# Second attention of a two-attention block: scores query-major, P turned by DMA

## The reference, cut to what matters

```python
# x: (2, 1024, 128) f32, so B = 2 batches, S = 1024 tokens, E = 128
x = x + attn_a(layernorm(x))        # 16 heads of 64, causal
x = x + ffn(layernorm(x))           # relu(h @ w1 + b1) @ w2 + b2, width 512
x = x + attn_b(layernorm(x))        # the part that the change touches
x = x + ffn(layernorm(x))           # the same weights again

def attn_b(x):                      # one head, E = 128
    scores = einsum('bqe,bke->bqk', x @ W_qk, x) / sqrt(128)
    scores = scores + (kpos - qpos) * alibi_slope          # linear bias
    scores = where(qpos >= kpos, scores, -inf)             # causal
    attn = softmax(scores, axis=-1)
    return einsum('bqk,bkd->bqd', attn, x @ W_v.T)
```

## Time and profile before

| | |
|---|---|
| median of 3 runs | 562.55 us |
| span of the profiled execution | 561.3 us |
| instructions | 17932 |
| PE busy | 526.3 us (94%) |
| DVE busy | 446.3 us (80%) |
| ACT busy | 469.0 us (84%) |
| POOL busy | 453.8 us (81%) |
| mean granted TensorE clock | 0.988 |

### The profile page before, as it was taken

The page is one execution under the profiler, slowest core; times in us unless marked ns, Lnnn a source line. Parts: engine busy times, 40 slices in busy tenths (PEclk is TensorE's granted clock), DMA queues, the critical chain, the costliest instruction groups (busy, mean ns, idle before and its releaser), DMA issues.

```text
span 561.3 us, 17932 instructions
## 1 busy us (share of the span) xinstructions
PE 526.3 (94%) x6864; PEld 371.1 (66%) x6864; DVE 446.3 (80%) x1382; ACT 469.0 (84%) x925; POOL 453.8 (81%) x447
## 2 busy tenths in 40 slices
PE   4888999999999999999999999998989998798897
PEld 3654666666666666766667666675679695656576
DVE  5878888888888888888888888887785575788943
ACT  3888998999988999989999899998973978573995
POOL 5678989888888888888888888888983977654885
PEclk9979999999999999999999999999999999998999
DMA  9442343332433324333243332435147100000002
GB/s 227 109 113 57 72 110 86 96 96 68 114 87 97 95 64 118 87 95 96 60 122 80 102 97 58 124 78 198 40 151 272 68 3 2 1 1 2 1 21 57
DMA packets 35461, 48.03 MB, mean 86 GB/s; under 512 B 10777, under 2 KB 16817, under 8 KB 35377
## 3 DMA queue, kind: packets, MB, share of 16 engines
q1 hardware_dynamic: 33264, 46.35, 30.2%
q10 hardware_dynamic: 2112, 0.54, 0.4%
HBM read 12.27 MB, written 9.44 MB: 39 GB/s over the span
## 4 chain that ended last, share of the span: by engine, by line
PE 75%; DVE 8%; issue 6%; ACT 5%; POOL 5%; DMA 1%; DVEq 0%; POOLq 0%; ACTq 0%
PE psum L562 11%; PE psum L620 10%; PE psum L621 10%; PE psum L516 7%; PE psum L518 6%; PE psum L517 6%; PE psum L600 6%; PE psum L602 6%; PE psum L601 6%; PE psum L623 2%; POOL h_lo L2146 1%; PE psum L781 1%; POOL rstd L2024 1%; ACT xn L1164 1%; DVE st_lo L1515 1%
## 5 line engine op out<-in xcount | busy, mean ns | idle before, releaser
L2079 POOL TENSOR_TENSOR p_hl<-p,p_hl 128x512 f16<-128x512 f32 x288 | 328.5, 1165 | 48.4 <-ACT p_hl L1264 44.6
L1532 DVE CUSTOM_DVE_ANT_0 max_junk<-psum,mask_s 128x1024 bf16<-128x1024 f32 (+7 forms) x256 | 190.4, 753 | 32.7 <-issue 32.6
L1263 ACT ACTIVATE p<-psum 128x512 f32<-128x512 f32 x288 | 175.9, 611 | 13.8 <-PE psum L623 12.2
L1264 ACT ACTIVATE p_hl<-psum 128x512 f16<-128x512 f32 x288 | 177.2, 615 | 0.0
L620 PE MATMUL psum<-q_hl,k_hh 128*128 128x512 f16 (+3 forms) x384 | 125.6, 327 | 0.5 <-ACT p_hl L1264 0.4
L600 PE MATMUL psum<-v_all,p_hl 128*128 128x65 f16 x1152 | 124.8, 193 | 1.1 <-POOL p_hl L2079 1.0
L601 PE MATMUL psum<-v_all,p_hl 128*128 128x64 f16 x1152 | 124.9, 192 | 0.0
L602 PE MATMUL psum<-v_all,p_hl 128*128 128x65 f16 x1152 | 124.4, 194 | 0.0
L621 PE MATMUL psum<-q_hm,k_l 128*128 128x512 f16 (+3 forms) x384 | 122.3, 327 | 0.0
L600 PEld LDWEIGHTS psum<-v_all,p_hl 128*128 128x128 f16 x1152 | 107.1, 98 | 16.1 <-POOL p_hl L2079 1.2
L601 PEld LDWEIGHTS psum<-v_all,p_hl 128*128 128x128 f16 x1152 | 106.2, 97 | 4.8
(11 more groups left out here) (206 smaller groups left out, 1109.1 us busy)
## 6 DMA issues: line engine op xcount, KB each, us to landing
k_hh<-st_hi SPq DMA_DIRECT2D x64, 128.0 KB, 2.3
o_scratch<-o_sb SPq DMA_DIRECT2D x16, 512.0 KB, 2.6
o_in<-o_scratch SPq DMA_DIRECT2D x8, 1024.0 KB, 8.6
q_hl<-st_hi SPq DMA_DIRECT2D x32, 128.0 KB, 2.4
q_hl<-st_lo SPq DMA_DIRECT2D x32, 128.0 KB, 2.4
k_l<-st_lo SPq DMA_DIRECT2D x32, 128.0 KB, 2.3
q_hm<-st_hi SPq DMA_DIRECT2D x32, 128.0 KB, 2.4
x_sb<-in_L_attn_a_x SPq DMA_DIRECT2D x4, 256.0 KB, 3.9
```

What stands on the lines that cost most here:

```text
L1263: nc.scalar.activation(p32[:, ring_at(u, r), :], src, ACT.Exp, scale=SCALE_A).then_inc(exp_done, 1)
L1264: nc.scalar.activation(p_hl[:, u % 2, 0, BANK * r:BANK * (r + 1)], src, ACT.Exp, scale=SCALE_A).then_inc(phi_done, 1)
L1532: nc.vector.tensor_tensor_reduce(out=max_junk[:, n % 2, 0:cols], in0=max_banks(v, j, 0, cols), in1=mask_s[:, S - cols:S], scale=1.0, scala ...
L2079: nc.gpsimd.tensor_tensor(p_hl[:, u % 2, 1, cols], p32[:, ring_at(u, r), :], p_hl[:, u % 2, 0, cols], ALU.subtract)\
```

## The change

The second attention makes its scores once, query-major, in three passes (row j of 128 queries against its 128(j+1) keys, in the banks of ROW_BANKS). `take_row_b` is the former reduce, but keeps its elementwise output, score plus bias, in a ring of three f32 rows (rows32); a one-column operation negates and scales the maximum. `exponentials_b` works on a row, with the negated maximum as per-partition bias and the score scale as per-partition scale: first the float16 high half into p_rows, then, in place, the f32 value. `low_b` writes the low half beside the high one, and one DMA transpose per row, issued from SP, turns both halves into pt_b, keys on the partitions. `outputs_b` reads that. The maxima pass, the transposed maxima, k_one, qm_b, bias_t and `biased` are gone. All four lists of calls are written anew for this part; the calls per engine are the same otherwise.

```diff
+    ROW_BANKS = (3, 4, 3, 4, 5, 3, 5, 3, 5, 6, 5, 6, 3, 3, 3, 3)
+    ROW_AFTER = (0, 0, 1, 2, 0, 4, 5, 6, 7, 7, 9, 10, 8, 13, 14, 15)
+    ROW_RING, MOVE_RING = 3, 4
@@ sync, between the loads of the first attention's output and the result stores
+            for m in range(B * QT):
+                j, slot = m % QT, m % MOVE_RING
+                sp.wait_ge(plob_done, m + 1)
+                sp.dma_start_transpose(pt_b[:, m // QT, j * (j + 1):(j + 1) * (j + 2), :], p_rows[:, slot, 0:2 * P * (j + 1)])\
+                    .then_inc(row_moved[slot], 16)
@@ tensor
+            def scores_b(b, j):
+                m = QT * b + j
+                if j % CT == 0:
+                    pe.wait_ge(qb_lo_done, m // CT + 1)
+                if m == 0:
+                    pe.wait_ge(ot_lo_done, OB * CHUNKS)
+                if m == CT:
+                    pe.wait_ge(h_hi_done, FW * CHUNKS)
+                if ROW_AFTER[m]:
+                    pe.wait_ge(row_done, ROW_AFTER[m])
+                rows, cols = slice(P * m, P * (m + 1)), P * (j + 1)
+                for c0 in range(0, cols, BANK):
+                    c1 = min(c0 + BANK, cols)
+                    keys = slice(S * b + c0, S * b + c1)
+                    last = three(psum[:, BANK * ROW_BANKS[m] + c0:BANK * ROW_BANKS[m] + c1], qb_hi[:, rows], qb_lo[:, rows], xT_hi[:, keys], xT_lo[:, keys])
+                last.then_inc(row_full, 1)
             def outputs_b(b, j):
-                        pe.wait_ge(plob_done, NU * b + need_units[j])
+                        pe.wait_ge(row_moved[m % MOVE_RING], 16 * (m // MOVE_RING + 1))
...
@@ scalar
+            def exponentials_b(b, j):
+                m, cols = QT * b + j, P * (j + 1)
+                slot = m % MOVE_RING
+                act.wait_ge(row_turned, m + 1)
+                if m >= MOVE_RING:
+                    act.wait_ge(row_moved[slot], 16 * (m // MOVE_RING))
+                src = rows32[:, m % ROW_RING, 0:cols]
+                nc.scalar.activation(p_rows[:, slot, 0:cols], src, ACT.Exp, bias=neg_max[:, m:m + 1], scale=score_scale[:, 0:1]).then_inc(phib_done, 1)
+                act.wait_ge(phib_done, m + 1)
+                nc.scalar.activation(src, src, ACT.Exp, bias=neg_max[:, m:m + 1], scale=score_scale[:, 0:1]).then_inc(expb_done, 1)
@@ vector
+            def take_row_b(b, j):
+                m, cols = QT * b + j, P * (j + 1)
+                dve.wait_ge(row_full, m + 1)
+                if m >= ROW_RING:
+                    dve.wait_ge(plob_done, m - ROW_RING + 1)
+                nc.vector.tensor_tensor_reduce(out=rows32[:, m % ROW_RING, 0:cols], in0=psum[:, BANK * ROW_BANKS[m]:BANK * ROW_BANKS[m] + cols], in1=bias_s[:, S - cols:S],
+                                               scale=1.0, scalar=-3.0e38, op0=ALU.add, op1=ALU.max,
+                                               accum_out=max_b[:, b, j:j + 1]).then_inc(row_done, 1)
+                dve.wait_ge(row_done, m + 1)
+                nc.vector.tensor_scalar(neg_max[:, m:m + 1], max_b[:, b, j:j + 1], score_scale[:, 0:1], -1.0, ALU.mult, ALU.mult).then_inc(row_turned, 1)
@@ gpsimd
+            def low_b(b, j):
+                m, cols = QT * b + j, P * (j + 1)
+                pool.wait_ge(expb_done, m + 1)
+                nc.gpsimd.tensor_tensor(p_rows[:, m % MOVE_RING, cols:2 * cols], rows32[:, m % ROW_RING, 0:cols], p_rows[:, m % MOVE_RING, 0:cols],
+                                        ALU.subtract).then_inc(plob_done, 1)
```

More of the change, by code:

```diff
@@ L1109, in _ @@
             hidden(4, 2)
+            hidden(4, 3)
+            scores_b(1, 7)
             outputs_b(1, 4)
-            hidden(4, 3)
+            hidden(5, 0)
+            hidden(5, 1)
+            forward(4, 0)
+            forward(4, 1)
             outputs_b(1, 5)
-            hidden(5, 0)
-            outputs_b(1, 6)
-            hidden(5, 1)
-            outputs_b(1, 7)
-            turn_late(ln_of[3, 2])
-            forward(4, 0)
             hidden(5, 2)
             hidden(5, 3)
-            forward(4, 1)
             forward(4, 2)
             forward(4, 3)
+            outputs_b(1, 6)
+            turn_late(ln_of[3, 2])
+            outputs_b(1, 7)
             hidden(6, 0)
@@ L1925, in _ @@
             late_stats(ln_of[2, 2])
-            take_max_b(0, 6)
+            take_row_b(0, 5)
             add_result(7, 0)
+            take_row_b(0, 6)
             add_result(7, 1)
-            take_max_b(0, 7)
             late_stats(ln_of[2, 3])
-            max_rows_b(0)
-            values_low(1)
             chunk_low(ln_of[2, 2])
-            biased(0, 0)
-            biased(0, 1)
+            take_row_b(0, 7)
             queries_low(2)
-            biased(0, 2)
-            chunk_low(ln_of[2, 3])
@@ L1957, in _ @@
-            take_max_b(1, 6)
-            take_max_b(1, 7)
             outputs_out_b(0, 3)
-            max_rows_b(1)
             late_stats(ln_of[3, 0])
-            biased(1, 0)
-            biased(1, 1)
+            chunk_low(ln_of[2, 3])
+            values_low(2)
             outputs_out_b(0, 4)
-            biased(1, 2)
+            queries_low(3)
+            take_row_b(1, 0)
+            take_row_b(1, 1)
             outputs_out_b(0, 5)
+            values_low(3)
+            take_row_b(1, 2)
@@ L1967, in _ @@
+            take_row_b(1, 3)
             outputs_out_b(0, 6)
-            biased(1, 3)
-            biased(1, 4)
+            take_row_b(1, 4)
+            chunk_low(ln_of[3, 0])
             outputs_out_b(0, 7)
             late_stats(ln_of[3, 1])
-            biased(1, 5)
-            biased(1, 6)
+            take_row_b(1, 5)
             outputs_out_b(1, 0)
-            biased(1, 7)
-            chunk_low(ln_of[3, 0])
             outputs_out_b(1, 1)
+            take_row_b(1, 6)
             outputs_out_b(1, 2)
-            biased(1, 8)
@@ L2221, in _ @@
             hidden_low(2, 2)
+            low_b(0, 0)
+            low_b(0, 1)
             add_forward_row(2)
             hidden_low(2, 3)
+            low_b(0, 2)
             hidden_low(3, 0)
             hidden_low(3, 1)
+            low_b(0, 3)
             hidden_low(3, 2)
```

287 lines of the change are left out of this document (88 added, 199 removed).

## The result

The changed kernel took **582.2 us** (581.8 to 582.9, 4 runs), 562.6 before: ratio 1.0361, interval 1.0339 to 1.0382. Slower, as forecast (572.5), but by 19.6 us and not 10, and 2.2 us outside the range. The profiled execution has a span of 580.5 us (561.3 before) and a mean granted clock of 0.976 (0.988).

A forecast was written before the change was run, and what follows sets the result against it. From 475 us no engine is full; waits, mostly ScalarE's two holes, bound it, and row (1,7) sets the end. Last norm 10.5 us later, 17.8 instead of 18.3 behind it: 562.55+10.0 = 572.5 us, range 556 to 580.

The forecast's parts named there:

- Pairs at 0.92+0.21j: ScalarE's two exponentials per row j, high half then f32 value in place, priced in us: 26.5 for 16 rows.
- Step (a): Start on ScalarE: norm(1,3), behind queries_high(1) and the first exponential pair, starts at 475.1, 3.5 us late.
- (d): Batch 0: GpSimd has low_b(0,4) ahead of rstd(2,2), putting norm(2,2) at 497.4; before it was 487.16.
- rival A: ScalarE stays fed: both big holes go, last norm at 537.8, -5.7 us, 557 us; chance 0.2.
- (b): Batch 0: exponential (0,3), its maximum queued behind results waiting for hidden tiles, starts 485.5; ScalarE was free at 483.6.
- (c): Batch 0: scores(0,4) uses a hidden bank and waits for the last hidden tile; exponential (0,4) from 492.1 to 493.9.
- (e): Batch 0: low_b ahead of rstd again, through exponential (0,7); norm(3,0) at 518.6, against 516.99 before the change.
- (f): Batch 1 on ScalarE: pairs, copy and hidden tiles up to pair (1,5), then norm(3,1) at 529.6, against 527.40.
- (g): Batch 1 on ScalarE: from norm(3,1) to the end of pair (1,7), with 1 us of hand-overs: 541.7.
- (h): Last row's tail: low_b 2.4, transpose 3.5, passes and drain 1.6, output 0.8; last norm 553.5, 10.5 us later.
- Rival B: SP's transposes are the bound: at 8.6 us per 2048 rows they take 77 us, 577.5 us; chance 0.12.
- The reserve of the forecast: Behind the last norm: no backlog of chunk 5 on GpSimd, so 17.8 us instead of 18.3.

The follow-up runs named there:

- e8: The changed kernel with 60 idle products on TensorE before the last outputs, to keep its clock up: 580.7 us.
- e6: The changed kernel with norm [1,3] first and batch 1 reordered: last rows ahead of hidden tiles, chunk 4's forward calls behind the last outputs: 572.2 us.
- e11: e9 without its 40 idle products, with scores and maximum of row (1,5) and hidden tile (4,0) ahead of the outputs of row (0,7): 569.7 us.
- e3: The changed kernel with the last rows of batch 1 ahead of chunk 5's hidden tiles, two forward calls of chunk 4 still ahead of the last outputs: 582.2 us.
- e4: The changed kernel with each transpose replaced by an ordinary DMA of the same bytes (output isn't attention): 579.4 us.
- e10: e9 with constants for the exponentials' bias and scale instead of pointers (values not the softmax's): 572.1 us.
- e1: The changed kernel with one ScalarE call moved: norm [1,3] ahead of queries_high(1) and the first exponential pair: 578.7 us.
- e2: The changed kernel with batch 0's statistics ahead of GpSimd's low halves, and the calls feeding them moved earlier on the other engines: 581.9 us.
- e9: e6 plus the moves of e2, a ring of five rows before the transposes, and 50 and 40 idle products on TensorE: 572.9 us.

## Why the prediction was right and where it was wrong

Right: the direction, and the main mechanism, waits written into the order. ScalarE's idle time near 20 us (19.9). Pairs at 0.92+0.21j (for j = 7 2.39; measured 543.99 to 546.51, 2.52). The 15 pairs from 475 us on are 26.7 us busy. Step (a) 474.75 for 475.1, (d) with GpSimd's low half ahead of the statistics, 499.15 for 497.4. VectorE's reduce kept its time with f32 output. The transposes held up single rows only, though two of them, not (1,7) alone; rival A was never near: norm [3,1] at 533.1, not before 522.

Wrong, in the profiled execution 9.2 us (580.5 for 571.3), of which:

| step | forecast | measured | adds |
|---|---|---|---|
| (b), (c): exponentials (0,3), (0,4) | 485.5, 492.1 | 486.23, 493.74 | 1.6 |
| (d), (e): norm [3,0] | 518.6 | 520.98 | 0.8 |
| (f): norm [3,1] | 529.6 | 533.08 | 1.1 |
| (g): last exponential ends | 541.7 | 546.5 | 1.3 |
| (h): its low half ends | + 2.4 | + 4.4 | 2.0 |
| (h): transpose lands | + 3.5 | + 4.3 | 0.8 |
| (h): passes, drain, output to x_sb | + 2.4 | + 3.6 | 1.2 |
| (h): x_sb to last norm | + 3.57 | + 3.4 | -0.2 |
| behind the last norm | 17.8 | 18.3 | 0.5 |

The steps that failed are "low_b 2.4" in (h), the price of TensorE's passes all along the walk, and the hand-overs in (b) to (g). (Rival B's 577.5 us lies nearer to the 582.2 measured than the forecast does; that is luck, since its mechanism isn't there.)

In (h) I went along ScalarE and started the low half when its source was ready, though my own list of GpSimd's order has two hidden tiles and the statistics of [3,2] ahead of it: it began 2.2 us late, 0.3 by the tiles and 2.0 by the statistics.

I read the distance of TensorE's passes from a stretch in which it had been busy and used it everywhere, behind long waits too. In the trace some of them ran at the lower clock. That cost 1.2 us in the 24 passes of row (1,7) (e8), and in the walk 0.8 us in the scores of row (0,4) and 1.1 in the chunk behind norm [3,1], by comparison with e8, whose code is the same there. So 1.9 of the 4.8 us of (b) to (g) are clock. These 1.9 are what one trace of each kernel shows.

Another 0.5 of the 4.8 is a slip: the terms of (f) add up to 530.05 and not to 529.6, since the hand-overs of 0.5 named there were not added. What is left, 2.4 us, is longer pairs (2.52 for 2.39) and small waits for a turn or a product where I had counted busy time only, some of them at the lower clock too. No run isolates these one by one, and how they share the 2.4 stays open. That order can give back more than was missed is shown by e6 and e11, which leave every operation of the rows as it is and give back 12.5 us (582.2 to 569.7), e11 with the ring of five and 50 idle products. The prices in the forecast were not what was missed, but for the transpose: 4.3 us for 3.5, a size and not a mechanism. (The smallest transfer is 64 KB, not the 32 of the prediction; nothing rests on it.)

The Trainium skill, "Advanced Engine Details and Errata" (X-Bar Transpose), has the transfer as fast as an ordinary one. Here it isn't: 4.3 us against 2.9 for the same 512 KB. The 1309 ns that the Trainium skill, "VectorE: DVE Perf Modes" (The three transpose paths), gives for one block can't be added up block by block either, since the 16 blocks of a full row landed within 4.3 us.

The reserve of the forecast, 17.8 behind the last norm because no backlog would stand on GpSimd, didn't come: 18.3 as before, and never less in any of the twelve runs (19.0 to 19.5 in e3, e4, e6, e8 and e10). So what stood on GpSimd had probably not been part of that stretch's chain; no run tests it.

## What to carry to other kernels

Walk a new order engine by engine, and for the last item write down everything ahead of it in each queue that it crosses; an item is late by the longest of these queues, not by the one that you follow. In a pipeline that is bounded by waits, the saving of one wait may only move it to the next in-order call of another engine: e1 moved one call and gained 3.5 us, but e2 and e3 moved several lists and gained little or nothing, and with the forward calls moved as well e3's order gave 6.5 us over e1. Before such a rewrite is tuned, run its floor (the disputed operations at their cheapest, the best order known): here 563.7 us said that there was nothing to win in the orders tried. And before a difference of a microsecond between two traces is put down to an edit, compare them ahead of the edit, the granted clock first: in e4 and e8 1 to 2 us were there before it.

## What was not expected of the hardware

- A DMA transpose of float16 halves within SBUF (64 to 512 KB) took 2.4, 3.4, 4.3 us to landing (least, median, most), 0.6 to 1.4 more than the plain copies' 1.8 to 2.9 (e4), and kept SyncE's queue 1.2 to 1.8 us for its issue, where a plain copy kept it 0.5.
- A pointer for scale and one for bias cost 0.18 us per activation at every width here: 1.25 for 1.07 at 1024 columns, 0.49 for 0.31 at 128. It is a fixed price, so it weighs on short rows.
- TensorE's passes of row (1,7), behind a 4 us wait, ran at 0.11 instead of 0.057 apart, at a granted clock of 0.50, the lower of the two levels, 1.2 GHz. Idle products in the wait kept the distance at 0.057 (e8); where there was no wait they cost 2.0 us (e9).
- A wait of the same length did not always end at the same level: behind 4.03 us in the same code, the scores of row (0,4) ran at 0.50 in the changed kernel's trace and at 1.00 in that of e8.
